# Attention inside a two-layer block: heads change places in half of each window, the 64-row products use all four array positions, the head outputs lie in two banks, and each step is ordered by array mode

## What is computed

```python
SEGMENT_LENGTH = 64; DILATION_RATE = 4; NUM_HEADS = 16; HEAD_DIM = 64
seg = pos // SEGMENT_LENGTH
local = seg[None, :] == seg[:, None]
diff = abs(pos[None, :] - pos[:, None])
dil = (diff > 0) & (diff % 4 == 0) & (diff <= 256)
mask = where(local | dil, 0, -inf)
q, k, v = (x_norm @ w).reshape(B, S, H, Dh)          # for w_q, w_k, w_v
scores = einsum('bqhd,bkhd->bhqk', q, k) * Dh ** -0.5 + mask
out = einsum('bhqk,bkhd->bqhd', softmax(scores), v).reshape(B, S, H * Dh)
x = x + out @ w_o
```

## Time and profile before

| | |
|---|---|
| time, median of 3 runs (range) | 480.57 us (476.65 to 482.73) |
| span of the profiled execution | 478.9 us |
| TensorE matmuls busy | 448.3 us, 94% |
| TensorE weight loads busy | 351.4 us, 73% |
| VectorE busy | 403.7 us, 84% |
| ScalarE busy | 331.6 us, 69% |
| GpSimd busy | 297.0 us, 62% |
| DMA queue 1, share of 16 engines | 34.8%, 38.38 MB |
| the step loop of the attention | about 57 to 312 us of the span |

### The profile page before, as it was taken

The page is one execution under the profiler, slowest core; times in us unless marked ns, Lnnn a source line. Parts: engine busy times, 40 slices in busy tenths (PEclk is TensorE's granted clock), DMA queues, the critical chain, the costliest instruction groups (busy, mean ns, idle before and its releaser), DMA issues.

```text
span 478.9 us, 17292 instructions
## 1 busy us (share of the span) xinstructions
PE 448.3 (94%) x6440; PEld 351.4 (73%) x6440; DVE 403.7 (84%) x1368; ACT 331.6 (69%) x972; POOL 297.0 (62%) x501
## 2 busy tenths in 40 slices
PE   6899989999999999999999999999878879989995
PEld 4678768888887887887888788877544746558674
DVE  5987759987998898889898688897999998998674
ACT  3477858878777768768778767865653687986433
POOL 4134638777577668668668567548478897572222
PEclk9899999999999999999999999999998999999999
DMA  6278682355344344345464645443000000000002
GB/s 219 110 215 245 166 270 51 73 114 118 74 95 94 73 93 95 72 94 116 87 135 100 138 96 106 83 87 67 1 0 0 2 0 1 1 2 1 1 0 89
DMA packets 136099, 40.54 MB, mean 85 GB/s; under 512 B 104976, under 2 KB 131024, under 8 KB 136016
## 3 DMA queue, kind: packets, MB, share of 16 engines
q1 hardware_dynamic: 135440, 38.38, 34.8%
q10 hardware_dynamic: 576, 1.05, 0.6%
HBM read 29.44 MB, written 9.96 MB: 82 GB/s over the span
## 4 chain that ended last, share of the span: by engine, by line
PE 59%; SPq 9%; POOL 9%; DVE 8%; DMA 6%; ACT 5%; issue 3%; ACTq 0%; POOLq 0%; DVEq 0%
PE psum L416 10%; PE psum L458 9%; PE psum L1181 5%; PE psum L478 5%; PE psum L492 4%; PE psum L504 4%; PE psum L489 4%; PE psum L397 4%; SPq L285 3%; PE psum L1176 3%; PE psum L399 2%; PE psum L398 2%; DMA st<-w_rows_dram 2%; DMA w_rows_dram<-st 2%; POOL rs L1899 2%
## 5 line engine op out<-in xcount | busy, mean ns | idle before, releaser
L942 POOL TENSOR_SCALAR pband<-pband,fac 128x192 f32<-128x192 f32 x256 | 104.1, 427 | 85.6 <-DVE fac L758 85.5
L562 ACT ACTIVATE pband<-pband,st 128x192 f32<-128x192 f32 x256 | 113.2, 448 | 0.1
L706 DVE CUSTOM_DVE_ANT_0 pband<-psum,band_mask 128x192 f32<-128x192 f32 x256 | 76.2, 353 | 1.0 <-PE psum L416 0.9
L416 PE MATMUL psum<-keys,q_class 64*64 64x192 f32 (+2 forms) x1536 | 66.5, 275 | 0.5 <-issue 0.5
L458 PEld LDWEIGHTS psum<-ident,pband 128*128 128x128 f32 x384 | 45.2, 141 | 21.6 <-issue 13.6
L416 PEld LDWEIGHTS psum<-keys,q_class 64*64 64x64 f32 x1536 | 57.6, 133 | 3.4 <-issue 2.6
L458 PE MATMUL psum<-ident,pband 128*128 128x128 f32 x384 | 53.2, 274 | 2.6 <-DVE pt L767 2.6
L562 ACT ACTIVATION_READ_ACCUMULATOR pband<-pband,st 128x1 f32 x256 | 49.5, 193 | 0.0
L924 POOL COPY keys<-k_rows 128x512 f32<-128x512 f32 x32 | 36.2, 1132 | 19.0 <-issue 10.7
L767 DVE COPY pt<-psum 128x512 f32<-128x512 f32 x64 | 43.7, 683 | 2.1 <-PE psum L458 1.9
L932 POOL COPY q_class<-q_rows 128x512 f32<-128x512 f32 x32 | 36.3, 1134 | 11.3 <-ACT q_rows L602 11.3
(11 more groups left out here) (221 smaller groups left out, 1103.6 us busy)
## 6 DMA issues: line engine op xcount, KB each, us to landing
v_rows_dram<-arena SPq DMA_DIRECT2D x32, 256.0 KB, 3.5
v_both<-v_rows_dram SPq DMA_DIRECT2D x32, 256.0 KB, 3.7
v_seg<-v_rows_dram SPq DMA_DIRECT2D x64, 128.0 KB, 3.6
v_side<-v_rows_dram SPq DMA_DIRECT2D x96, 64.0 KB, 2.6
w_rows_dram<-st SPq DMA_DIRECT2D x64, 8.0 KB, 2.9
st<-w_rows_dram SPq DMA_DIRECT2D x64, 8.0 KB, 2.5
arena<-_attn_hidden_states_dram SPq DMA_DIRECT2D x4, 256.0 KB, 3.6
out_dram<-x SPq DMA_DIRECT2D x4, 256.0 KB, 2.5
```

What stands on the lines that cost most here:

```text
L416: return pe.matmul(bank[2 * r + head][rows, at:at + y.shape[1]], x, y, start=True, stop=True, skip_group_check=True)
L562: act.activation(x, x, ACT.Exp, bias=mine[:, head:head + 1], scale=-1.0, accum_out=mine[:, 2 + head:3 + head]).then_inc(s_exp, 1)
L706: dve.tensor_tensor_reduce(pband[:, G % P_SLOTS, c, head, :], bank[2 * r + head][:, at:at + BAND], band_mask[:, (0, 1, 1, 2)[w], SEG * (1 ...
L942: pool.tensor_scalar(x, x, fac[:, F % 2, 1, c, head:head + 1], 1.0, ALU.mult, ALU.mult).then_inc(s_scaled, 1)
```

## The change

- **Places.** `place(head, half)` is head XOR half. In the score banks, in the turned blocks and in `v_side`, the two heads change places in the second half of the queries of a class; in the segment part, they change in the tiles 2 and 3. The positions in the array of a weighing product are then four, not two. `v_seg` holds both heads on both halves of the partitions, so its two DMAs per unit bring 256 KB each in place of 128 KB.
- **Banks.** Each weighing writes two banks (`half_bank`), one for each half of the queries. The output projection and the projected queries share one of them (`mixed_bank`), the projected keys the other (`row_bank`); the table of occupants is used in the prologue alone. `take_out` reads both.
- **Class weighing.** The 8 products of 128 columns with b = 0 and 1 become 16 of 64.
- **Order in a step.** TensorE: output, turns 0 and 1, both projections, turns 2 and 3, then all weighing, then all scores. The turns are now all of unit t - 6. The scores with r = 0 include the segment tiles of both halves, and wait for every maximum of the unit before; inside the scores there are two waits of TensorE on itself (`s_band`, `s_late`). VectorE and ScalarE handle maxima, exponentials and sums of unit t - 3, and differences t - 5, one step later than before. The loop has one step more, and rounding the weights (`quantise`) begins two steps later.

The diff, cut to its core:

```diff
         v_both = sb("v_both", [P, DIL, NW, P])
         v_side = sb("v_side", [P, DIL, 2 * (NW - 1), DH])
-        v_seg = sb("v_seg", [P, T // SEG, DH])
-    turn_bank, out_bank, shared_bank = bank[4:6], bank[6], bank[7]
+    turn_bank, half_bank = bank[4:6], bank[6:8]
+    mixed_bank, row_bank = half_bank
-    DRAIN = NS_ALL + 1
+    DRAIN = NS_ALL + 2
-    for t in range(FIRST_STEP, NS_ALL + 8):
-        occupants += [(t - lag, who) for who, lag in (("key", 0), ("wo", 7), ("query", 0)) if there(t - lag)]
...
+    def query_bank(t):
+
+        return row_bank if t < FIRST_STEP else mixed_bank
+
+    def wait_rows(pe, x, name):
+
+        if x >= FIRST_STEP:
+            if name == "query":
+                wait(pe, s_acc, x - FIRST_STEP)
+            else:
+                pe.wait_ge(*(shared_reader(FIRST_STEP - 1, "query") if x == FIRST_STEP else (s_out, x - FIRST_STEP)))
+            return
         at = occupants.index((x, name))
         if at:
             pe.wait_ge(*shared_reader(*occupants[at - 1]))
 
+    def place(head, half):
+
+        return head ^ half
+
     def seg_scores(r):
+    def by_class(half):
+
+        return half_bank[half][:, 0:WT // 2].rearrange("q (x c) -> q c x", c=DIL)
 
...
                     sp.dma_start(v_seg[DH * head:DH * (head + 1), 2 * TW * w:2 * TW * (w + 1), :],
-                                 v_rows[WT * w:WT * (w + 1), P * p + DH * head:P * p + DH * (head + 1)].rearrange(
+                                 v_rows[WT * w:WT * (w + 1), P * p:P * (p + 1)].rearrange(
                                      "(s x) f -> x s f", x=SEG)).then_inc(s_v[w], 16)
-                        sp.dma_start(v_side[DH * head:DH * (head + 1), :, side, :],
+                        at = place(head, side % 2)
+                        sp.dma_start(v_side[DH * at:DH * (at + 1), :, side, :],
                                      v_rows[DIL * SEG * (side + 1):DIL * SEG * (side + 2),
...
-                wait(pe, s_max, 8 * (G - 1) + 4 * (r + 1))
-                wait(pe, s_seg, 2 * (G - 1) + r + 1)
-                first, second = slice(0, SEG), slice(SEG, P)
-
-                def product(head, rows, at, x, y):
-                    return pe.matmul(bank[2 * r + head][rows, at:at + y.shape[1]], x, y, start=True, stop=True,
-                    product(0, second, at, x0[:, second], y0[:, SEG:SEG + BAND])
-                    product(1, first, at, x1[:, first], y1[:, 0:BAND])
-                    product(0, first, at, x0[:, first], y0[:, SEG:BAND])
-                    product(1, second, at + SEG, x1[:, second], y1[:, SEG:BAND])
-                    product(0, first, at + P, x0[:, first], y0[:, 0:SEG])
-                    product(1, second, at, x1[:, second], y1[:, BAND:BAND + SEG])
...
-                            last = product(head, rows, at, q_rows[dims, G % ROW_SLOTS, cols],
-                                           k_rows[dims, G % ROW_SLOTS, cols])
+                wait(pe, s_max, 8 * G if r == 0 else 0)
+                wait(pe, s_seg, 2 * G if r == 0 else 0)
+                halves = slice(0, SEG), slice(SEG, P)
+
+                def product(head, half, at, x, y):
+                    rows = halves[half]
+                    return pe.matmul(bank[2 * r + place(head, half)][rows, at:at + y.shape[1]], x[:, rows], y, start=True,
+                                     stop=True, skip_group_check=True)
+                        product(1, 1, at, x1, y1[:, SEG:SEG + BAND])
+                        product(1, 0, at, x1, y1[:, 0:BAND])
+                        product(0, 0, at, x0, y0[:, SEG:BAND])
+                        product(0, 1, at + SEG, x0, y0[:, SEG:BAND])
+                        product(0, 0, at + P, x0, y0[:, 0:SEG])
+                        last = product(0, 1, at, x0, y0[:, BAND:BAND + SEG])
...
+                if r == 0:
+                    classes().then_inc(s_band, 1)
+                    segments(1).then_inc(s_late, 1)
+                    pe.wait_ge(s_band, G + 1)
+                    last = segments(0)
+                else:
+                    pe.wait_ge(s_late, G + 1)
+                    last = classes()
                 last.then_inc(s_score, 1)
 
...
+                    if U + FIRST_STEP < NS_ALL:
+                        pe.wait_ge(s_key, U + FIRST_STEP + 1)
+                        pe.wait_ge(s_query, U + FIRST_STEP + 1)
+                    else:
+                        pe.wait_ge(s_acc, U)
...
+                    c, at = 2 * b + k // 2, k % 2
+                    for half in range(2):
+                        head = place(at, half)
                         dims = slice(DH * head, DH * (head + 1))
-                        last = pe.matmul(by_class[dims, c, :], v_both[:, c, w, dims], turned[:, P * k:P * (k + 1)],
+                        last = pe.matmul(by_class(half)[dims, c, :], v_both[:, c, w, dims],
+                                         turned[:, P * k + SEG * half:P * k + SEG * (half + 1)],
                                          start=(b == 0 and k < 2), stop=False, skip_group_check=True)
...
+            def weigh_sides(U):
+
...
+                for k in range(4):
+                    for half, side in enumerate((2 * w - 2, 2 * w + 1)):
...
                         for head in range(2):
+                            dims, at = slice(DH * head, DH * (head + 1)), place(head, half)
+                            rows = slice(DH * at, DH * (at + 1))
+                            last = pe.matmul(by_class(half)[dims, k, :], v_side[rows, k, side, :],
+                                             turned[rows, P * k + SEG * half:P * k + SEG * (half + 1)],
+                                             start=False, stop=False, skip_group_check=True)
+                last.then_inc(s_pv[0], 1)
...
+            def weigh_segments(U):
...
+                for a in range(TW // 2):
+                    for s in range(2):
+                        for half in range(2):
+                            k = TW // 2 * half + a
+                            for head in range(2):
+                                dims, at = slice(DH * head, DH * (head + 1)), place(head, half)
+                                rows = slice(DH * at, DH * (at + 1))
+                                last = pe.matmul(half_bank[half][dims, P * a + SEG * s:P * a + SEG * (s + 1)],
+                                                 v_seg[rows, 2 * (TW * w + k) + s, dims],
+                                                 turned[rows, P * k + SEG * s:P * k + SEG * (s + 1)], start=False,
+                                                 stop=(a == 1 and s == 1), skip_group_check=True)
+                last.then_inc(s_pv[1], 1)
...
-                wait_shared(pe, U, "wo")
                 pe.wait_ge(s_out, U + 1)
-                pe.matmul(shared_bank[:, :], wo[:, U // NW, :], o_sb[:, :], start=True, stop=True).then_inc(s_mix, 1)
+                pe.matmul(mixed_bank[:, :], wo[:, U // NW, :], o_sb[:, :], start=True, stop=True).then_inc(s_mix, 1)
...
             for t in range(FIRST_STEP, DRAIN):
+                output(t - 7)
+                turn(t - 6, 0)
+                turn(t - 6, 1)
                 project(t, 1)
+                project(t, 0)
+                turn(t - 6, 2)
+                turn(t - 6, 3)
                 weigh(t - 6, 0)
                 weigh(t - 6, 1)
-                turn(t - 6, 3)
-                output(t - 7)
-                turn(t - 5, 0)
-                weigh(t - 6, 2)
+                weigh_sides(t - 6)
+                weigh_segments(t - 6)
                 scores(t - 2, 0)
-                weigh(t - 6, 3)
                 scores(t - 2, 1)
-                project(t, 0)
-                turn(t - 5, 1)
-                turn(t - 5, 2)
...
             for t in range(FIRST_STEP, DRAIN):
-                exp_difference(t - 4)
+                exp_difference(t - 5)
+                band_exps(t - 3, 0)
+                odd_turned(t - 6, 1)
+                take_keys(t)
+                take_queries(t)
+                odd_turned(t - 6, 3)
+                band_exps(t - 3, 1)
+                seg_exps(t - 3)
                 take_out(t - 6)
-                take_queries(t)
-                odd_turned(t - 5, 1)
-                take_keys(t + 1)
-                band_exps(t - 2, 0)
-                odd_turned(t - 5, 3)
-                seg_exps(t - 2)
-                band_exps(t - 2, 1)
...
             for t in range(FIRST_STEP, DRAIN):
-                differences(t - 4)
-                even_turned(t - 5, 0)
-
+                differences(t - 5)
+                band_max(t - 3, 0)
+                factors(t - 5)
+                accumulate(t - 7)
+                even_turned(t - 6, 0)
+                seg_max(t - 3, 0)
+                band_max(t - 3, 1)
+                even_turned(t - 6, 2)
+                seg_max(t - 3, 1)
                 if t in (7, 8):
...
                 if QUANT_STEP <= t < QUANT_STEP + 15:
                     quantise((t - QUANT_STEP) // 5, (t - QUANT_STEP) % 5)
```

(9 more changed lines are left out.)

138 lines of the change are left out of this document (69 added, 69 removed).

## The result

The changed kernel takes **516.79 us** (median of 4 runs, 515.75 to 518.01); the kernel before, timed beside it, 480.82 (476.65 to 482.73). The ratio is 1.076 with an interval of 1.071 to 1.080: 36 us slower. The forecast was 469.5 with a range to 482, so its sign was wrong. Where a few executions of a kernel fell into a slower state of the chip, times and ratios here are of the others.

What follows compares the result with a forecast made beforehand. TensorE was taken to bound the loop at 9.03 us per step, 8.5 after with paths through TensorE and ScalarE taking turns. Gains of 11.1 us gave a 467.8 span, plus 1.7: 469.5 us, range 461 to 482.

Steps and rivals of the forecast that it cites:

- TensorE's price: Step loop: four positions bring sides, segments and scores from 3.81 to 2.8 us; TensorE's step sums to 8.25 us.
- the sum: Whole kernel: 8.5 us from 16 steps, 2.5 from 8, 1.0 from the last 2, -0.9 at the end; 11.1 together.
- the rival with 39 us: TensorE's weighing and band scores: row halves take turns at a shared bank, 39 us more, 520; chance 0.05.
- I cost it at nothing: VectorE's weight rounding: at most two 0.5 us operations in 15 steps, covered by its wait for the segment exponential.
- GpSimd ... stays covered: Step loop: GpSimd has 6.5 us per step and its results are needed a step later, so it adds nothing.
- SyncE and the exchange: The 8 steps with side loads, where v_seg brings twice the bytes: 8.8 us per step instead of 9.09, 2.5 in all.
- the rival: SyncE's queue: doubled v_seg loads make the statistics' round trip set the step, 9.6 us each, 15 us more, 495; chance 0.09.
- Edges: Loop entry and end: entry level, give or take 1.5 us; 0.9 us lost at the end through unit 29's factors.
- Level, give or take 1.5: Loop entry: the send of unit 5 comes out level with the kernel before, give or take 1.5 us.

Runs made afterwards that it cites:

- before_q_late: The kernel before with the rounding moved from ahead of the factors to ahead of the segment sums: 491.9 us, 1.025.
- closing: Changed kernel with GpSimd's query copy waiting for the differences, wo loaded earlier, both heads of v_seg in the first pair only (computation incomplete): 498.5 us, 1.039.
- pool_split: Changed kernel with one more wait: GpSimd copies the queries by class only after VectorE has taken the next step's differences: 511.6 us, 1.064.
- new_order: Changed kernel with wo earlier, turn 0 between the score groups, VectorE's turned block, segment maximum, accumulation and rounding ahead of the factors: 533.4 us, 1.110.

## Why the prediction was wrong

- **TensorE's price: right.** Sides, segments and scores came to 3.0 us against the 2.8 expected, the undisturbed step 8.46 against 8.25 to 8.5. The classes of a group, with banks shared by both row halves, take 0.69 us (240.62 to 241.31) against the 0.66 of the sum and the 1.33 of the rival with 39 us, which was rightly given little. That rival followed the rule in the Trainium skill ("TensorEngine Tiling (Array Packing)", Restrictions and Gotchas, Gotcha 1) that different row tiles cannot access the same bank at the same time; the trace does not agree with it here.
- **"I cost it at nothing": this step failed.** I took each rounding operation as 0.5 us wherever it stood, and looked only for idle time on VectorE to put it in. But that idle time lies beside GpSimd's work, and there the first operation takes 2.0 to 2.5 us in 12 of the 15 steps (in the other three it is a reduce, and the one behind it takes 1.5). In the kernel before, this alone costs 12 us (`before_q_late`). The Trainium skill ("SBUF — State Buffer", Who interferes with whom) states a rule for it: a VectorE instruction with two SBUF inputs, or in a 2-port mode, is held up for the whole of a GpSimd instruction that has the shared port pair, while a reduce never is. The rows above agree as to which instructions are held up, also with 0.19 us for the reduce L801 beside 2.16 for L805. They differ in how long: in nearly all cases VectorE got in only at the end of GpSimd's back-to-back stretch, past boundaries between its instructions. A wait for one instruction would be 1.2 us here at most; the wait to the end of the stretch is what makes the cycle of 9.8 us and more in the steps with rounding.
- **"GpSimd ... stays covered": failed with it.** Its results are early enough, but while it works it holds up VectorE's operations on SBUF operands. The stretch of 6.4 us was there before; the new order puts such operations beside it. The loop of factors, GpSimd, sums, differences, maxima is one that I had not drawn.
- **SyncE and the exchange: the direction was right only in the rival.** I took 8.8 per step for the doubled loads and gave the rival 0.09. (8 steps at 8.8 in place of 9.09 are 2.3 us, where the sum has 2.5.) The loads cost 9 us in the kernel before by late statistics. In the changed one they cost 10, but there the waits for statistics were short, and what fell without them is the idle time without a releaser.
- **TensorE's instructions: not in the sum.** It stops 18 times, 23 us in all, nearly always in the dense run of 64-row products. The Trainium skill ("Runtime: NRT & Kernel Launch", Instruction fetch mechanics) has the fetching of 16 KB blocks as mostly hidden; the kernel before agrees (0.5 us of idle time), and this one does not, if its stops are late blocks as the pattern says.
- **Edges: failed.** "Level, give or take 1.5" overlooked `wo` and the output's place at the top of the step: unit 4's segment maximum comes 3.9 us later, unit 5's 5.4. From unit 31's segment maximum to the end it is 168.6 us against 165.0, 3.6 more where I had 0.9.

What stays open: the losses cover each other, so their single prices do not add up to 36 us. Of the last 18 us (`closing` against the kernel before) the cause is not shown; its profile has 15.6 us of idle time on TensorE without a releaser, and is 1.9 us late at unit 4. The whole price of the hold-up in the changed kernel is not known either: `pool_split` took 1.1 of the 6.4 us out of the way and gave 5 us, and `new_order`, which alone has the rounding clear of GpSimd's work, put the difference beside it. The share of the lower clock was not tested. Two more things were not separated: whether late blocks come from the density of the run or from how the block edges fall in it, and what of the 10 us for the loads goes through the blocks.

## What to carry to other kernels

Before an operation is moved into another engine's idle time, look at what the third engine does just then: beside a busy GpSimd, VectorE's operations whose operands all lie in SBUF, reduces aside, can last until GpSimd's stretch ends. Draw the cycles of an order with these hold-ups as edges, and check each expected step against every cycle, because several of nearly equal length hide each other and mending one gives little or nothing. When small instructions come to stand closer together, look at the landing of instruction blocks. Count small DMAs ahead of a latency-bound one in the same queue as well as their bytes.
